# Local attention layers of a mixed transformer on Trainium2: inverse norms, rotary sum, value copies and turned probabilities moved between engines

## The reference, cut to what matters

```python
def attn_layer(x, Wqkv, qs, ksc, Wo):       # 16 heads of 64, window 32
    q, k, v = split_heads(x @ Wqkv)
    q = l2norm(q) * qs                      # t / max(norm(t), 1e-12) for each token and head
    k = l2norm(k) * ksc
    q = q * cos * scale + rotate_half(q) * sin * scale
    k = k * cos * inv + rotate_half(k) * sin * inv
    sim = einsum('...ie,...je->...ij', q, look(k)) * 8   # own window of 32 tokens and the one before
    out = einsum('...ij,...je->...ie', softmax(where(mask, -inf, sim)), look(v))
    return out @ Wo

def ffn_layer(x, g, bln, W1, b1, W2, b2):
    xn = layernorm(x) * g + bln
    a, gate = split(xn @ W1 + b1)
    return a * gelu(gate) @ W2 + b2
x = shift_tokens(x)                         # before each of the two, and both are added to the state
```

## Time and profile before

| | us |
|---|---|
| runs before | 2541.15, 2540.86, 2536.29 |
| median of the three | 2540.86 |
| the profiled execution, its own time | 2539.16 |
| its span, first to last instruction | 2537.4 |
| outside the span | 1.8 |
| from the first to the last `negmax` of the local layers | 529.6 to 2176.4 |
| busy in the span: PE, DVE, ACT, POOL | 2410.0, 1996.4, 1882.4, 1765.7 |

### The profile page before, as it was taken

The page is one execution under the profiler, slowest core; times in us unless marked ns, Lnnn a source line. Parts: engine busy times, 40 slices in busy tenths (PEclk is TensorE's granted clock), DMA queues, the critical chain, the costliest instruction groups (busy, mean ns, idle before and its releaser), DMA issues.

```text
span 2537.4 us, 98073 instructions
## 1 busy us (share of the span) xinstructions
PE 2410.0 (95%) x36438; PEld 1707.4 (67%) x36442; DVE 1996.4 (79%) x4388; ACT 1882.4 (74%) x6630; POOL 1765.7 (70%) x1605
## 2 busy tenths in 40 slices
PE   7999888879999999999999999999999999799999
PEld 6888555546666666666766666666666766377874
DVE  5555699978888888888888888888888888555644
ACT  4777799868888888888888888888888888533323
POOL 1888888488888888888888878888888888122200
PEclk9999999999999999999999999999999999899999
DMA  4001210021112111211112111211121111100000
GB/s 123 15 15 15 51 14 14 10 85 36 32 34 67 38 36 33 58 42 42 34 45 55 42 32 34 66 39 36 34 58 42 42 33 34 30 1 1 1 1 17
DMA packets 177876, 91.06 MB, mean 36 GB/s; under 512 B 40974, under 2 KB 174328, under 8 KB 177408
## 3 DMA queue, kind: packets, MB, share of 16 engines
q1 hardware_dynamic: 168574, 80.42, 11.8%
q0 software_dynamic: 8192, 4.21, 1.4%
q10 hardware_dynamic: 642, 0.15, 0.0%
HBM read 30.57 MB, written 3.76 MB: 14 GB/s over the span
## 4 chain that ended last, share of the span: by engine, by line
PE 82%; DVE 9%; issue 5%; POOL 2%; ACT 1%; SPq 0%; DMA 0%; DVEq 0%; POOLq 0%; ACTq 0%
PE bank L1191 13%; PE bank L1208 9%; PE scores L1243 7%; PE bank L1254 7%; PE bank L1198 6%; PE scores L1225 6%; PE bank L1180 3%; PE bank L1283 3%; PE bank L1301 2%; PE bank L639 2%; PE bank L1292 2%; PE scores L1219 2%; DVE rg_prod L1011 2%; PE scores L671 2%; PE bank L1925 1%
## 5 line engine op out<-in xcount | busy, mean ns | idle before, releaser
L1627 POOL TENSOR_TENSOR rs<-ssc,neg_half 128x8 f32<-128x8 f32 x384 | 643.5, 1676 | 38.9 <-DVE ssc L1447 38.9
L1617 POOL TENSOR_TENSOR t_pair<-qn_pair,tabs 128x512 f32<-128x512 f32 x384 | 488.7, 1273 | 12.3 <-DVE qn_pair L1435 11.6
L1555 ACT ACTIVATE pr<-scores,negmax 128x64 f32<-128x64 f32 x1536 | 460.3, 311 | 48.8 <-DVE negmax L1455 23.9
L1607 POOL TENSOR_TENSOR pr<-pr,rec 128x256 f32<-128x256 f32 x384 | 235.1, 612 | 282.4 <-DVE rec L1427 282.4
L1191 PE MATMUL bank<-wqk,xs 128*128 128x512 f32 x768 | 402.5, 606 | 12.4 <-DVE qn_pair L1435 11.3
L1555 ACT ACTIVATION_READ_ACCUMULATOR pr<-scores,negmax 128x1 f32 x1536 | 311.1, 203 | 0.0
L1083 POOL DMA_INDIRECT rg_win<-rg_images,share_down x256 | 256.6, 1002 | 70.3 <-issue 55.2
L1443 DVE TENSOR_REDUCE ss<-sq 128x8 f32<-128x512 f32 x384 | 260.9, 679 | 33.4 <-ACT sq L1578 32.4
L1435 DVE TENSOR_TENSOR qn_pair<-bank,rs 128x512 f32<-128x512 f32 x384 | 257.1, 670 | 27.1 <-POOL rs L1627 26.9
L1546 ACT COPY vt<-bank 128x256 f32<-128x256 f32 x361 | 135.1, 374 | 188.0 <-issue 186.9
L1208 PE MATMUL bank<-oT,wo 128*128 128x128 f32 x1536 | 266.2, 296 | 0.0
(11 more groups left out here) (313 smaller groups left out, 5503.2 us busy)
## 6 DMA issues: line engine op xcount, KB each, us to landing
rg_prod<-vt SPq DMA_DIRECT2D x1536, 32.0 KB, 1.9
wqk<-in_L_ffn_Wqkv SPq DMA_DIRECT2D x20, 256.0 KB
rg_win<-rg_images,share_down POOLq DMA_INDIRECT x256
wv<-in_L_ffn_Wqkv SPq DMA_DIRECT2D x20, 128.0 KB
wo<-in_L_ffn_Wo SPq DMA_DIRECT2D x20, 128.0 KB
w<-in_L_ffn_W SPq DMA_DIRECT2D x6, 341.0 KB
rg_images<-rg_prod SPq DMA_DIRECT2D x1, 1625.0 KB, 8.6
ZT<-in_x SPq DMA_DIRECT2D x4, 256.0 KB, 4.1
```

The source lines that it names most:

```text
L1555: ex = act.activation(pr[t % 2][:, h * BAND:(h + 1) * BAND], sl_ps[:, h // 2, h % 2 * BAND:(h % 2 + 1) * BAND], ACT.Exp, bias=negmax[t % 2 ...
L1617: pool.tensor_tensor(t2[t % 2][:, :].rearrange("p (i h f e) -> p i h f e", i=2, h=GH, f=2), qn[t % 2][:, :].rearrange("p (i h f e) -> p i ...
L1627: pool.tensor_tensor(rs[t % 2][:, :], ssc[t % 2][:, :], neg_half[:, 0:8], ALU.pow)\
```

## The change

Five things are changed, all in the local layers:

1. **Inverse norms.** POOL's power over 128x8 is replaced, except in burst slots, by two activations on ACT at the head of the following slot: `Ln` of the sums, then `Exp` with scale -0.5, with a semaphore (`logged`) between them. One set of tables that has both functions is loaded explicitly, at the start of the local layers and behind each burst, in place of the activation `unread`. In burst slots POOL's power stays.
2. **Rotated halves.** The 128x512 addition `qr` goes from DVE to the head of POOL's slot.
3. **Values.** The copy of the values is always DVE's, one slot earlier, just before the row maxima; the values have four buffers instead of three.
4. **Probabilities first.** PE's `turn_probs` comes before `queries`.
5. **Their copy.** ACT's copy of the turned probabilities stands between the second and the third exponential instead of behind the fourth.

```diff
--- before
+++ after
...
@@ -72 +74 @@
-L_QKV, L_ROPE, L_COS, L_SUM, L_TURN, L_SCORE, L_V, L_MOVE, L_EXP, L_PROB, L_PROJ = 1, 2, 3, 4, 5, 6, 5, 6, 7, 8, 9
+L_QKV, L_ROPE, L_COS, L_SUM, L_TURN, L_SCORE, L_V, L_EXP, L_PROB, L_PROJ = 1, 2, 3, 4, 5, 6, 5, 7, 8, 9
@@ -556,7 +559,7 @@
             sp.dma_start(m_rank[:, :], d["c_rank"]).then_inc(s.m_loaded, 16)
             for t in range(LOCAL + 32):
                 if live(t):
-                    near, far = vt[t % 3], vx[t % 2]
+                    near, far = vt[t % GROUPS], vx[t % 2]
                     sp.wait_ge(a.v_moved, TICKS + t + 1)
                     sp.wait_ge(a.o_ready, TICKS + t - 1)
                     if t >= 2:
@@ -1141,6 +1144,8 @@
 
             return ffn_step(u)[1] == F_GELU
 
+        LOGS = list(itertools.accumulate(0 if bursts(t + L_QKV) else 1 for t in range(LOCAL)))
+
         def types_dve(dve, part):
             step_no = [0 if part == 0 else 4 + TYPES]
 
@@ -1304,10 +1309,10 @@
 
             pe.wait_ge(s.wqkv_loaded, 16 * 10)
             def slot(u):
+                if live(u - L_PROB):
+                    turn_probs(u - L_PROB, u)
                 if live(u - L_QKV):
                     queries(u - L_QKV)
-                if live(u - L_PROB):
-                    turn_probs(u - L_PROB, u)
                 for t in projections(u, 0):
                     project(t)
                 if live(u - L_TURN):
@@ -1399,15 +1404,6 @@
                     dve.tensor_tensor(ZT[:, at], yl_ps, ZT[:, at], ALU.add).then_inc(a.added, 1)
 
             tables(0)
-            def turned(t):
-                if live(t):
-                    dve.wait_ge(a.roped_c, t + 1)
-                    dve.wait_ge(a.roped_s, t + 1)
-                    if t >= 2:
-                        dve.wait_ge(a.qkT_ready, t - 1)
-                    dve.tensor_tensor(qr[t % 2][:, :], t1[t % 2][:, :], t2[t % 2][:, :], ALU.add)\
-                        .then_inc(a.qr_ready, 1)
-
             def cosines(t):
                 if live(t):
                     l = t // TICKS
@@ -1484,7 +1480,6 @@
                 add(u - 1 - L_PROJ)
                 if u in (TYPED, TYPED + FFN_EVERY):
                     types_dve(dve, u // (TYPED + 1))
-                turned(u - L_SUM)
                 cosines(u - L_COS)
                 if bursts(u - 1):
                     normed(u - L_ROPE)
@@ -1497,15 +1492,16 @@
                     dve.wait_ge(a.qkT_ready, t + 1)
                     dve.wait_ge(a.sc_ready, TICKS + t - 1)
                     dve.tensor_copy(qkT[t % 2][:, :], turn_ps[:, :]).then_inc(a.qkT_moved, 1)
-                t = u - L_V
-                if live(t) and bursts(u):
-                    dve.wait_ge(a.v_ready, TICKS + t + 1)
-                    dve.wait_ge(a.o_ready, TICKS + t - 2)
-                    dve.wait_ge(a.v_spread[(t - 3) % 2], 64 * ((t - 3) // 2 + 1))
-                    dve.tensor_copy(vt[t % 3][:, :], vl_ps).then_inc(a.v_moved, 1)
                 summed(u - L_QKV)
                 if u % TICKS == TICKS // 2 and u // TICKS + 1 < DEPTH:
                     tables(u // TICKS + 1)
+                t = u - L_V
+                if live(t):
+                    dve.wait_ge(a.v_ready, TICKS + t + 1)
+                    dve.wait_ge(a.o_ready, TICKS + t - 3)
+                    if t >= 4:
+                        dve.wait_ge(a.v_spread[t % 2], 64 * (t // 2 - 1))
+                    dve.tensor_copy(vt[t % GROUPS][:, :], vl_ps).then_inc(a.v_moved, 1)
                 maximum(u - L_SCORE, u)
             for u in range(TAIL):
                 slot(u)
@@ -1534,16 +1530,29 @@
                         w = FCH[j][1]
                         act.wait_ge(s.lf_gate, 3 * c + j + 1)
                         act.activation(gl[j][0:w, :], gl[j][0:w, :], ACT.Gelu).then_inc(s.lf_gelu, 1)
-                    act.activation(unread[:, :], xs[0][:, 0:1], ACT.Exp, scale=0.0)
+                    act.preload_act_table_set("natural_log_exp_and_others")
+
+            def pT_copy(u):
+                t = u - L_PROB
+                if live(t) and not bursts(u) and not bursts(u - 1):
+                    act.wait_ge(a.pT_ready, TICKS + t + 1)
+                    act.wait_ge(a.o_ready, TICKS + t - 1)
+                    act.copy(pT[t % 2][:, 0:GB], pTl_ps).then_inc(a.pT_moved, 1)
+
+            def inverse_root(t):
+                act.wait_ge(a.clamped, t + 1)
+                if t >= 2:
+                    act.wait_ge(a.normed, t - 1)
+                act.activation(rs[t % 2][:, :], ssc[t % 2][:, :], ACT.Ln).then_inc(a.logged, 1)
+                act.wait_ge(a.logged, LOGS[t])
+                act.activation(rs[t % 2][:, :], rs[t % 2][:, :], ACT.Exp, scale=-0.5).then_inc(a.rs_ready, 1)
+
+            act.preload_act_table_set("natural_log_exp_and_others")
 
             def slot(u):
-                t = u - L_MOVE
+                t = u - L_ROPE
                 if live(t) and not bursts(u - 1):
-                    act.wait_ge(a.v_ready, TICKS + t + 1)
-                    act.wait_ge(a.o_ready, TICKS + t - 2)
-                    if t >= 3:
-                        act.wait_ge(a.v_spread[(t - 3) % 2], 64 * ((t - 3) // 2 + 1))
-                    act.copy(vt[t % 3][:, :], vl_ps).then_inc(a.v_moved, 1)
+                    inverse_root(t)
                 t = u - L_EXP
                 if live(t):
                     act.wait_ge(a.negmax_ready, TICKS + t + 1)
@@ -1552,16 +1561,15 @@
                     if bursts(u - 1):
                         act.wait_ge(a.oT_moved, TICKS + u - L_PROJ + 1)
                     for h in range(GH):
+                        if h == GH // 2:
+                            pT_copy(u)
                         ex = act.activation(pr[t % 2][:, h * BAND:(h + 1) * BAND],
                                             sl_ps[:, h // 2, h % 2 * BAND:(h % 2 + 1) * BAND],
                                             ACT.Exp, bias=negmax[t % 2][:, h:h + 1],
                                             scale=1.0, accum_out=sums[t % 2][:, h:h + 1])
                     ex.then_inc(a.exp_ready, 1)
-                t = u - L_PROB
-                if live(t) and not bursts(u) and not bursts(u - 1):
-                    act.wait_ge(a.pT_ready, TICKS + t + 1)
-                    act.wait_ge(a.o_ready, TICKS + t - 1)
-                    act.copy(pT[t % 2][:, 0:GB], pTl_ps).then_inc(a.pT_moved, 1)
+                else:
+                    pT_copy(u)
                 t = u - L_PROJ
                 if live(t) and not bursts(u - 1):
                     b, g = t // GROUPS, t % GROUPS
@@ -1600,6 +1608,14 @@
 
         def pool_local(pool):
             def slot(u):
+                t = u - L_SUM
+                if live(t):
+                    pool.wait_ge(a.roped_c, t + 1)
+                    pool.wait_ge(a.roped_s, t + 1)
+                    if t >= 2:
+                        pool.wait_ge(a.qkT_ready, t - 1)
+                    pool.tensor_tensor(qr[t % 2][:, :], t1[t % 2][:, :], t2[t % 2][:, :], ALU.add)\
+                        .then_inc(a.qr_ready, 1)
                 t = u - L_EXP
                 if live(t):
                     pool.wait_ge(a.rec_ready, TICKS + t + 1)
@@ -1620,10 +1636,9 @@
                                        over(tabs[l % 2][:, :, :].rearrange("p i (f e) -> p i f e", f=2),
                                             [P, 2, GH, 2, HD // 2], 2), ALU.mult).then_inc(a.roped_s, 1)
                 t = u - L_QKV
-                if live(t):
+                if live(t) and bursts(u):
                     pool.wait_ge(a.clamped, t + 1)
-                    if t >= 2:
-                        pool.wait_ge(a.normed, t - 1)
+                    pool.wait_ge(a.normed, t - 1)
                     pool.tensor_tensor(rs[t % 2][:, :], ssc[t % 2][:, :], neg_half[:, 0:8], ALU.pow)\
                         .then_inc(a.rs_ready, 1)
                 c, step = ffn_step(u - 1)
```

4 lines of the change are left out of this document (3 added, 1 removed).

## The result

| | before | after |
|---|---|---|
| time, median of 4 runs | 2538.95 us (2536.29 to 2541.15) | 2559.33 us (2556.82 to 2559.66) |
| span of the profiled execution | 2537.4 us | 2554.8 us (its time: 2556.82) |
| ratio | | **1.0081, 95% interval 1.0068 to 1.0094** |

A forecast was written before the change was run, and what follows sets the result against it. PE was taken as full except in slots without a feed-forward product, where ACT and DVE's cycle would take over. +0.7 a turn times 23 = +16, -8 and +2 before the turns: +10, about 2550 us, range 2509 to 2578.

The forecast's parts named there:

- The second cycle, 3.74 to 4.08: ACT and DVE's loop from maxima to maxima: DVE's values copy adds 0.34 us, so it paces slots without feed-forward product.
- PE stays fed: Rival, chance 0.25: DVE's copy does not bind, the ACT and DVE cycle is 3.6 us or less; 2509 us.
- nothing to measure: Rival, chance 0.14: the losses behind the burst and at the chunk's copy are absorbed, the start gives 8; 2541 ± 5 us.
- the third rival: Chance 0.11: cosines held past `rec`'s start, or `Ln`, wait and `Exp` over 0.8 us; cycle 4.4, 2617 us.
- PE's head waits for the copy: At a slot's start `turn_probs` needs DVE's values copy, so PE may start 0.13 us after the maxima start (M).
- The cosines held at no cost: POOL's addition holds DVE's cosines by about 0.86 us, until M + 1.8, 0.26 before `rec` can go: costs nothing.
- (a): Steps 3 to 7 of a turn: from 16.42 us to 16.65, +0.2.
- (b): Steps 0 to 2 of a turn, with the chunk's copy on ACT: +0.1 us.
- (c): Step 9, with a product and no projection: 4.0 us becomes 4.08, and the burst's ACT chain starts from it: +0.1.
- (d): Behind the burst, where ACT is late: the copy brings the maxima 0.34 us later and holds PE's head, +0.3.
- Before the turns: First ticks without POOL's power take 2.6 to 3.2 us, not 4.12: -8; the 12 quiet slots behind them: +2.
- The change, part by part: The section pricing each moved piece of work within a slot, such as DVE's copy, 0.34 us between `ssc` and the maxima.

The follow-up runs named there:

- values_dve: Kernel before with only the copy of the values moved to DVE before the row maxima, four buffers and the explicit table load: ratio 1.0056.
- copy_twice: Changed kernel with the values copied twice on DVE, the first time into a tile that nothing reads: ratio 1.0341 to the kernel before.
- act_copy: Changed kernel with values copied by ACT at its slot's end (DVE where ACT is late), addition left on POOL: ratio 1.0035 to the kernel before.
- add_dve: Changed kernel with the addition of the rotated halves back on DVE, ahead of the cosines: ratio 1.0120 to the kernel before.
- norms_only: Kernel before with only the inverse norms changed, to `Ln` and `Exp` on ACT in place of POOL's power: ratio 1.0072.
- act_copy_add: Changed kernel with addition back on DVE and values copied by ACT at its slot's end (DVE where ACT is late): ratio 0.9988 to the kernel before.

## Why the prediction was right, and where it was off

2559.33 lies in the range of 2509 to 2578, on the side that I gave 0.55; it is 9 us above the 2550. That is less than it sounds: the forecast was +10 us and the kernel lost 20.4 by the medians, 17.4 by the spans, so about half of the loss was foreseen, and the range was wide enough for a gain of 30 as well. What carries the prediction is the mechanism, not the number.

**The second cycle, 3.74 to 4.08: right.** Measured 4.06 in the slot shown and 4.07 as median, with every station where the prediction put it: squares M + 2.13, `rec` M + 2.04 (2.06), `ss` M + 2.80. values_dve gives the same 4.07 without the other parts, copy_twice 4.41. The first rival, "PE stays fed", needed 3.6 or less and falls with these. So do "nothing to measure" and the slow pair of the third rival: the pair took 0.24 from start to start and 0.45 in all, where I took 0.5.

**PE's head waits for the copy: right.** It starts at M + 0.23 and not M + 0.13: behind the copy's end come some 0.15 (1189.14 behind 1188.57 + 0.42, and 1185.08 behind a copy of 1184.51), where I had 0.05, which no row gave. The idle time at L1185 with `vt` as its releaser is on the page.

**The cosines held at no cost: right here, for the reason given.** They lose 0.89 of 1.02 us overlap and end at M + 1.90, 0.14 before `rec`; predicted were 0.86, M + 1.8 and 0.26. The prediction's own terms make 0.34 + 0.68 + 0.86 = 1.88 and a cover of 0.18, so the slip is in its sum, and the trace is close to its terms. The cover lies in these slots alone. The prediction said that without it each us is added; act_copy and the tables showed both.

**The sum of a turn: +0.7 predicted, +0.82 measured.** (a) into steps 4 to 7: 16.42 to 16.76, +0.34 for +0.2. Its three quiet slots take 4.20 + 4.07 + 4.07 = 12.34, as worked out; the miss is step 7, where I let PE win back 0.22 and it won nothing (4.42). (b) into steps 1 to 3: +0.16 for +0.1. (c) step 9: +0.12 for +0.1. (d) steps 10 and 11: 9.64 to 9.88, +0.24 for +0.3. Times 23 that is 19 and not 16.

**Before the turns:** -7.4 by slot 9 for -8, and +2.3 for +2 over the slots to 25. The first ticks come at 2.0 to 3.5 us (the starts of `sq`: 508.78, 510.82, 514.32, 517.58, 521.00), in three of four steps over the 2.6 to 3.2. The cosines are held there, 1.11 to 1.45 in four of the first five, as the upper end supposed; what adds the last 0.1 to 0.3 I didn't follow.

**The step that failed: "The change, part by part" left out the tables.** The sum prices 16 steps of a turn, and the five slots with an extra piece on DVE have no term in it, so they stood at nothing without a reason. The new copy stands behind that piece, and so does PE's head. The two slots cost 0.32 more than a usual pair before, and 10.34 - 8.85 = 1.49 after: 1.17, times 5 = **+5.9**. About half of it comes from the hold: add_dve, with nothing on POOL to hold the tables, pays 9.82 - 8.96 = 0.86 for them. The rest is there without the hold, with the copy now behind the tables. The rows on it were there to be read: in the trace of before the three products stand between `ssc` and the maxima (L1342 at 1188.32 and L1345), inside the very turn of the earlier trace rows, whose 69.2 is the 69.00 of a common turn and some 0.3 for them.

The sum as measured: -7.4 + 2.3 + 18.7 (22.8 turns by 0.82) + 5.9 = 19.5, and the last maxima are 19.3 later (2195.7 and 2176.4). Behind them 1.9 comes back, which no term had; values_dve has it too (14.6 at the last maxima, 12.7 in the span). I didn't follow where.

**POOL waits for `rec`: right,** 421.6 us of idle time, 282.4 before. That 19% of the chain runs through POOL I read as a tie: in the slot shown its addition ends at 1184.93 + 1.27 = 1186.20, just when PE comes to turning the queries. values_dve and add_dve have no addition on POOL, and their quiet slots are the same.

**What may take the shared port.** In the Trainium skill, "SBUF — State Buffer", section "Who interferes with whom", the list of what can take the shared pair also has `tensor_scalar`, when it runs in a two-port mode, and not only instructions with two inputs. I had cited only the second. The trace agrees with both as to who is held: the scaling, one tensor input, took 1.19 for 0.55 (in which mode it ran, no view here shows). As a full lock the rule gives an end at 834.61 + 0.55 = 835.16; the record ends at 834.90, 0.26 earlier. For the cosines it is 1186.88 by the lock and 1186.75 in the record. So both holds were shorter than a lock for the whole instruction gives, and the measurement decides.

The measurement also differs from the rule on POOL's side. In the kernel before, POOL's power reads two SBUF tiles too, but it held none of the cosines:

```profile
898.49 1.64 POOL L1627 TENSOR_TENSOR rs<-ssc,neg_half 128x8 f32<-128x8 f32 x1
```
```profile
899.35 0.68 DVE L1419 TENSOR_TENSOR t_pair<-qn_pair,tabc 128x512 f32<-128x512 f32 x1
```

In the local layers some 80 of the cosines lie wholly inside a record of the power, and all take 0.68 or 0.69. So the change took an instruction from POOL that held nobody and gave it one that does, which no term of the prediction says.

**What stays open:** why the parts don't add up (values_dve 0.56% and norms_only 0.72%, together with the rest 0.81%) is shown for the slots in which pair and copy stand ahead of the exponentials on ACT, but how much each of the four parts gives with each of the others wasn't run. Whether ACT could copy the values in the slots left to DVE in act_copy_add wasn't tried either.

## What to carry to other kernels

Find, beside the engine that is full, the next cycle through the semaphores, add it up from starts (not from busy times), and put a moved instruction in only where that cycle has slack: here 0.34 us on DVE, in an engine 79% busy, cost 0.56% alone. Then walk through the special slots too, the burst, the tables, the chunk copies: a moved instruction that comes to stand behind a rare piece of work waits for it, and so does all that needs it. And an instruction on an engine that shares a port has a price that depends on what runs under it, so that the same edit was worth -0.39% in one version and +0.47% in another.

## What the runs showed of the hardware

- `Ln` and `Exp` over 128x8 on ACT take 0.21 us each, and the second starts 0.24 after the first through a semaphore between them, 0.45 in all; the power of the same tile on POOL took 1.68. No table was loaded between them.
- An addition on POOL (128x512, two inputs, 1.27 us) held three kinds of DVE instruction: the cosines (0.68 to 1.57), the small products of the tables (0.35 to 1.42 for both, the first of them 1.28) and the scaling by a column (0.55 to 1.19). Row maxima, sums and copies from PSUM kept their lengths beside POOL's work (0.42, 0.69 and 0.42), and so did a 128x512 product with one of its two inputs in PSUM (L1369, 0.68 under the addition).
- POOL's power over 128x8 (1.64 us in the line shown above, two inputs; lengths on POOL are rough) held none of them: cosines 0.68, the tables' small products 0.21 each and the scaling 0.55 in the kernel before, all while it ran.
- A copy of 128x128 from PSUM took 0.29 on DVE and let the next instruction start 0.20 after its own start; 128x256 took 0.42 and 0.34. What counts in a sum is the second number.
